# A state-space and attention kernel: another order of PSUM banks, copies and softplus steps in its projection stage

## The chip, the cores and the metric

The kernel runs on one core of one Trainium2 chip. The metric is the device time of one execution in microseconds (us), as the median of several. An execution handles a batch of four images.

## What is computed

Every image has 128 channels of 64 x 64 pixels, so 4096 tokens of 128 values. Layer 0 scores and sorts patches, then runs a selective state-space model over the sorted tokens; layer 1 is attention and a mixture of eight experts. The change lies in the first part of the state-space model:

```python
xz = x1n @ in_proj_w.T
xm, z = (xz[..., :D_INNER], xz[..., D_INNER:])            # D_INNER = 256
xp = jnp.pad(xm.transpose(0, 2, 1), ((0, 0), (0, 0), (D_CONV - 1, 0)))
xc = jax.lax.conv_general_dilated(xp, conv1d_w[:, None, :], (1,), 'VALID', ...)   # 4 taps per channel
xc = jax.nn.silu(xc + conv1d_b[None, :, None]).transpose(0, 2, 1)
dbc = xc @ x_proj_w.T
dt = jax.nn.softplus(dt_low @ dt_proj_w.T + dt_proj_b)
dBx = dt[..., None] * Bc[:, :, None, :] * xc[..., None]   # the kernel's u is dt * xc
```

`silu(z)` is wanted later and made here too. Softplus is made as relu(v) + log(1 + exp(-|v|)), with a correction for what is rounded away when 1 is added.

## The kernel before

The program is a loop over the four images. For each it runs stages that end in a barrier of all engines: `score_and_sort`, `project`, `scan`, `unsort`, `qkv`, `attention`, `ffn`. A stage gives each engine its own list of instructions, executed in order; semaphores tie the lists together, and nothing reorders them. The change is in `project` (L631) and in one new helper.

`project` cuts the 4096 tokens into eight chunks of 512 columns. The 256 inner channels are two halves of 128 partitions, so most steps occur twice per chunk (`h` = 0, 1):

- TensorE: `inproj(c)` (L654) makes two matmuls for x into PSUM banks 0 and 1 and two for z into banks 2 and 3. `xproj(c)` (L647) makes two accumulating matmuls into bank 4. The trace lists an f32 matmul of this size as two passes, so a pair as four.
- ScalarE: `keep_xi(c)` (L677) copies the x banks into `xi` in SBUF, `silu_z(c)` (L688) makes Silu out of the z banks, `silu_x(c)` (L682) makes Silu of the convolved chunk, and `keep_dbc(c)` (L693) copies bank 4 into `dbc`. Before, the order is `keep_xi(c)`, `silu_x(c-1)`, `silu_z(c)`, `keep_dbc(c-1)`.
- VectorE: `convolve(c)` (L729) makes the four taps of each half, two multiplies (L735) and six multiply-adds (L738).

Each bank is reused for each chunk, so `inproj(c)` waits for the copies of chunk c-1 out of the same banks, and VectorE waits for the copies of its chunk.

For the first chunk only, the stage also makes what the scan needs at once. These steps are the methods of `Steps` (L535). ScalarE rounds a part of `dbc` ("high", L592, and "middle", L596), between which GpSimd makes the remainder (L611) and "low" (L615). TensorE makes the dt matmuls of both halves (`tensor_dt`, L568) into banks 5 and 6; ScalarE makes absolute value and Relu of each (L575, L576), the exponential (L580), adds one (L585), and, behind VectorE's `vector_rounding` (L601), the logarithm (L589). GpSimd then makes three sums and products of 1024 columns (`pool_softplus`, L621, L625, L628). Exp, Ln and Silu need different function tables of ScalarE; each switch is an `ACT_TABLE_LOAD`, some placed by `ready_table` (L103). Before, "high" stands behind chunk 1, "middle" behind chunk 2, the block from the table load to adding one behind chunk 3, and the logarithm behind chunk 5. The later chunks' softplus is made within the scan, with the same helpers, and is not changed.

```python
def body(c):
    keep_xi(c)
    silu_x(c - 1)
    silu_z(c)
    keep_dbc(c - 1)
```

Of the kernel before, what the change touches and what calls it, by code (L numbers as in the profile page):

```python
# [15 lines left out]
DI, DS, DR, DC = 2 * C, 16, C // 16, 4  # L16
HD = DI // 128
# [610 lines left out]
            pool.tensor_tensor(halves(self.u[q]), halves(self.dt[q]), self.xc[:, :, cols_of(c)], ALU.mult).then_inc(self.dt_s, 1)  # L628


def project(k):  # L631


    steps = Steps(k, (5, 6))
    nc = k.nc
    x1 = k.at(X1_AT, L)
    xc = k.at(XC_AT, HD * L).rearrange("p (h n) -> p h n", h=HD)
# [6 lines left out]
    with nc.Block() as block:  # L644
        @block.tensor
        def _(pe):
            def xproj(c):  # L647
                pe.wait_ge(xc_s, c * HD + HD)
                pe.wait_ge(xp_ev, c + 1)
                for h in range(HD):  # L650
                    last = pe.matmul(k.bank(4), k.xpw[:, h, :], xc[:, h, cols_of(c)], start=h == 0, stop=h == HD - 1)
                last.then_inc(xp_mm, 1)

            def inproj(c):  # L654
                for h in range(HD):
                    pe.wait_ge(xi_ev, c * HD + (h + 1))
                    pe.matmul(k.bank(h), k.wx[:, h * 128:(h + 1) * 128], x1[:, cols_of(c)], start=True, stop=True).then_inc(xi_mm, 1)
                for h in range(HD):
                    pe.wait_ge(z_ev, c * HD + (h + 1))
                    pe.matmul(k.bank(2 + h), k.wz[:, h * 128:(h + 1) * 128], x1[:, cols_of(c)], start=True, stop=True).then_inc(z_mm, 1)  # L660
# [12 lines left out]
            xproj(NCH - 1)  # L673

        @block.scalar
        def _(act):
            def keep_xi(c):  # L677
                for h in range(HD):
                    act.wait_ge(xi_mm, c * HD + (h + 1))
                    act.activation(xi[:, h, cols_of(c, CH, DC - 1)], k.bank(h), ACT.Copy).then_inc(xi_ev, 1)  # L680

            def silu_x(c):  # L682
                for h in range(HD):
                    act.wait_ge(tap_s, c * (HD * DC) + (HD * (DC - 1) + h + 1))
                    act.activation(xc[:, h, cols_of(c)], xc[:, h, cols_of(c)], ACT.Silu,
                                   bias=k.cols[:, C_CB + h:C_CB + h + 1]).then_inc(xc_s, 1)

            def silu_z(c):  # L688
                for h in range(HD):
                    act.wait_ge(z_mm, c * HD + (h + 1))  # L690
                    act.activation(sz[:, h, cols_of(c)], k.bank(2 + h), ACT.Silu).then_inc(z_ev, 1)

            def keep_dbc(c):  # L693
                act.wait_ge(xp_mm, c + 1)
                act.activation(dbc[:, cols_of(c)], k.bank(4), ACT.Copy).then_inc(xp_ev, 1)

            for s, n in ((xi_ev, HD), (z_ev, HD), (xp_ev, 1)):
                act.sem_inc(s, n)
            def body(c):
                keep_xi(c)  # L700
                silu_x(c - 1)
                silu_z(c)
                keep_dbc(c - 1)
# [15 lines left out]
            with act.Fori(4, NCH - 2) as c:  # L719
                body(c)  # L720
            steps.scalar_log(act, 0)
            body(NCH - 2)
            body(NCH - 1)
            silu_x(NCH - 1)
            keep_dbc(NCH - 1)

        @block.vector
        def _(dve):
            def convolve(c):  # L729
                dve.wait_ge(xi_ev, c * HD + (2 * HD))  # L730
# [971 lines left out]
```

## Time and profile before

| | us |
|---|---|
| median of 3 executions | 5907.59 (5905.54 to 5909.15) |
| the profiled execution, its own time | 5915.02 |
| its span in the profile | 5913.3 |
| VectorE busy in the span | 5095.8 (86%) |
| TensorE busy | 4687.3 (79%) |
| ScalarE busy | 3659.2 (62%) |
| GpSimd busy | 1753.6 (30%) |

Engines are PE (TensorE), PEld (its weight loads), DVE (VectorE), ACT (ScalarE), POOL (GpSimd) and SP (the DMA queue's engine). A line number such as L738 is that of the kernel before. In a timeline, consecutive like instructions are merged into one row: its start, the time from the first start to the last end, and in brackets the idle time of the engine before it with what ended it. Instructions of one engine may overlap by their latency, so the distance between two starts can be shorter than a duration.

### The profile page before, as it was taken

The page shows a single profiled execution, that of the slowest core. Times are in us where ns is not written, and L with a number is a line of the kernel's source. Part 1 is how long each engine was busy: PE and PEld are TensorE (multiplying, and loading weights), DVE is VectorE, ACT ScalarE, POOL GpSimd, SP SyncE. Part 2 cuts the span into 40 slices and gives each one's busy share as a digit, 9 for nine tenths or more (in the row PEclk, how much of TensorE's full clock was granted, in tenths as well). Part 3 has the DMA queues.
Part 4 walks back from the last instruction along what each step waited for, and adds up shares of the span by engine and source line. Part 5 has one row for each costly group of instructions (what it writes and reads, how often), then busy time and mean ns, then how long its engine had stood idle before and what let it go on. Part 6 is the DMA issues. An engine that isn't in the chain of part 4 may idle for free. (4 is left out here: it accounts for less than half of the span.)

```text
span 5913.3 us, 100635 instructions
## 1 busy us (share of the span) xinstructions
PE 4687.3 (79%) x33816; PEld 1950.2 (33%) x33880; DVE 5095.8 (86%) x6562; ACT 3659.2 (62%) x4769; POOL 1753.6 (30%) x1306
## 2 busy tenths in 40 slices
PE   5776779998667777999866677799986667779997
PEld 2222433333322243333432224333343222433334
DVE  6799769998779977999877997799986899679998
ACT  1666458883266646888326663688922666368892
POOL 3388600000148860000014885000001488500000
PEclk9899989999889998999888999899988899989998
DMA  1000020000000002000000000200000000020000
GB/s 38 0 1 0 15 62 9 9 5 22 22 0 1 0 15 62 9 9 5 22 22 0 1 0 15 62 9 9 5 22 22 0 1 0 15 62 9 9 5 15
DMA packets 41626, 87.14 MB, mean 15 GB/s; under 512 B 11672, under 2 KB 27872, under 8 KB 38112
## 3 DMA queue, kind: packets, MB, share of 16 engines
q1 hardware_dynamic: 41184, 81.11, 5.1%
q8 instruction: 294, 4.82, 0.3%
q14 instruction: 148, 1.21, 0.1%
HBM read 26.55 MB, written 8.39 MB: 6 GB/s over the span
## 5 line engine op out<-in xcount | busy, mean ns | idle before, releaser
L1271 ACT ACTIVATE arena<-ps 128x1024 f32<-128x1024 f32 x2048 | 1913.2, 1027 | 266.8 <-PE ps L1236 246.4
L1286 DVE TENSOR_TENSOR arena<-arena 128x1024 f32<-128x1024 f32 x1664 | 1904.7, 1216 | 42.7 <-ACT arena L1271 40.6
L916 DVE TENSOR_TENSOR_SCAN arena<-ps,hlast,arena 128x512 f32<-128x512 f32 x1024 | 1258.4, 1264 | 5.2 <-DVE arena L898 3.2
L876 POOL TENSOR_TENSOR arena<-arena 128x1024 f32<-128x1024 f32 x512 | 1206.3, 2356 | 22.6
L1236 PE MATMUL ps<-arena 128*32 128x512 f16 x16384 | 1096.7, 384 | 118.1 <-issue 92.9
L1219 PE MATMUL ps<-arena 128*32 128x512 f32 x8192 | 1079.6, 605 | 45.9 <-DVE arena L1291 38.1
L845 ACT ACTIVATE ps<-arena,amat 128x512 f32<-128x512 f32 x1024 | 691.9, 688 | 506.9 <-DVE arena L916 506.1
L813 PE MATMUL ps<-arena,ident 128*128 128x512 f32 x2048 | 973.1, 598 | 7.7 <-POOL arena L876 7.7
L1594 POOL MEMSET arena<- 128x1024 f32 x4 | 3.8, 956 | 2688.1 <-POOLq L101 2688.1
L1236 PEld LDWEIGHTS ps<-arena 128*32 128x32 f16 x16384 | 471.4, 98 | 974.3 <-issue 696.7
L898 DVE TENSOR_TENSOR arena<-arena,ps 128x1024 f32<-128x1024 f32 x512 | 609.9, 1191 | 50.3 <-remote 32.3
L813 PEld LDWEIGHTS ps<-arena,ident 128*128 128x128 f32 x2048 | 392.3, 193 | 344.9 <-issue 270.7
L821 PE MATMUL ps<-arena,sel 128*128 128x512 bf16 x448 | 178.7, 399 | 410.8 <-DVE arena L898 410.8
L1219 PEld LDWEIGHTS ps<-arena 128*32 128x32 f32 x8192 | 212.3, 109 | 467.5 <-ACT arena L1271 239.1
L821 PEld LDWEIGHTS ps<-arena,sel 128*128 128x128 bf16 x512 | 49.8, 97 | 802.8 <-DVE arena L898 747.1
L848 ACT ACTIVATE arena<-ps 128x512 f32<-128x512 f32 x512 | 297.6, 581 | 21.2 <-PE ps L825 20.4
L825 PE MATMUL ps<-arena,sel 128*128 128x512 bf16 x512 | 200.7, 392 | 101.5 <-ACT arena L576 41.5
L1640 DVE SCALAR_TENSOR_TENSOR arena<-ps,arena 128x128 f32<-128x128 f32 x1024 | 274.3, 342 | 1.6 <-PE ps L1545 0.3
L1545 PE MATMUL ps<-expw,arena 128*128 128x512 f32 x512 | 250.6, 615 | 11.1 <-DVE arena L1609 8.3
L462 PE MATMUL ps<-arena 128*128 128x512 f32 x512 | 233.7, 616 | 18.3 <-DVE arena L349 18.3
L873 POOL COPY hlast<-arena 128x2 f32<-128x2 f32 x512 | 117.1, 229 | 317.0 <-DVE arena L916 317.0
L1208 PE MATMUL ps<-arena,ones 128*32 128x512 f32 x1536 | 204.3, 604 | 3.1 <-DVE arena L1286 2.0
(242 smaller groups left out, 4409.5 us busy)
## 6 DMA issues: line engine op xcount, KB each, us to landing
arena<-x SPq DMA_DIRECT2D x32, 512.0 KB, 5.5
arena<-arena SPq DMA_DIRECT2D x64, 256.0 KB, 6.0
arena<-arena SPq DMA_DIRECT2D x64, 224.0 KB, 5.8
arena<-arena SPq DMA_DIRECT2D x28, 512.0 KB, 3.4
arena<-pe SPq DMA_DIRECT2D x256, 32.0 KB, 1.8
out<-arena SPq DMA_DIRECT2D x8, 1024.0 KB, 3.9
expw<-L_ffn_expert_w SPq DMA_DIRECT2D x1, 512.0 KB
wqkv<-L_attn_W_qkv SPq DMA_DIRECT2D x1, 192.0 KB
```

What stands on the lines that cost most here:

```text
L813: last = pe.matmul(k.bank(Y_BANK + h), k.ident[:, :], halves(g[s % 4])[:, h, :], start=False, stop=s == DS - 1)
L845: act.activation(da(s, h), halves(dt[q])[:, h, :], ACT.Exp, scale=k.amat[:, h, s:s + 1]).then_inc(da_s, 1)
L848: act.activation(cs[s % 4], k.bank(C_BANK), ACT.Copy).then_inc(cs_s, 1)
L876: pool.tensor_tensor(halves(g[s % 4]), halves(hb[s % 4]), cs[s % 4].unsqueeze(1).broadcast_to([128, HD, CH]), ALU.mult).then_inc(hc_s, 1)
L898: dve.tensor_tensor(halves(dbx[s % 2]), halves(u[q]), k.bank(B_BANK).unsqueeze(1).broadcast_to([128, HD, CH]), ALU.mult).then_inc(dbx_s, 1)
L916: dve.tensor_tensor_scan(halves(hb[s % 4])[:, h, :], da(s, h), halves(dbx[s % 2])[:, h, :], k.hlast[:, s, h, :], ALU.mult, ALU.add).then_i ...
L1219: last = pe.matmul(k.ps[32 * h:32 * h + 32, O * CH:(O + 1) * CH], v[:, j * 128 + 32 * h:j * 128 + 32 * h + 32], probs[(2 * j + h // 2) % 8 ...
L1236: last = pe.matmul(k.ps[32 * t:32 * t + 32, (2 * group[p] + e) * CH:(2 * group[p] + e + 1) * CH], ks[:, h, j * 128 + 32 * t:j * 128 + 32 * ...
L1271: act.activation(probs[p % 8], k.bank(2 * group[p], 2 * CH), ACT.Exp, scale=SCALE / SPLIT ** 2).then_inc(exp_s, 1)
L1286: dve.tensor_tensor(acc[p % 2], acc[p % 2], probs[p % 8], ALU.add).then_inc(acc_s, 1)
L1545: pe.matmul(k.bank(expert_bank(i, hb)), tnt[:, i * 128:(i + 1) * 128], k.expw[:, hb * HE:hb * HE + HE, :].rearrange("p e c -> p (e c)"), s ...
L1640: dve.scalar_tensor_tensor(tile, k.bank(expert_bank(i, hb), C, e * C), gate[:, i, hb * HE + e:hb * HE + e + 1], tile, ALU.mult, ALU.add).t ...
```

## The change

In `project`, TensorE's banks are given anew: the x matmuls alternate between two pairs of banks (0, 1 and 2, 3), z has 4 and 5, the x-projection 6, and both dt matmuls 7, the second behind the Relu of the first. ScalarE copies the x banks of chunk c+3 where it copied those of chunk c+1; all of the first chunk's softplus steps on ScalarE stand together behind the copy of chunk 5. The three last softplus steps go from GpSimd to VectorE, behind its eighth chunk; the rounding step stands behind chunk 5 where it stood behind chunk 4. The credits that ScalarE gave at the start go, and all loops over chunks are written out.

```diff
+    def vector_softplus(self, dve, c, q):
+        dve.wait_ge(self.ln_s, c + 1)
+        dve.tensor_tensor(self.onep, self.onep, self.ab, ALU.subtract).then_inc(self.l1_s, 1)
+        dve.wait_ge(self.l1_s, c + 1)
+        dve.wait_ge(self.rx_s, c * 2 + 2)
+        dve.tensor_tensor(self.dt[q], self.onep, self.rx, ALU.add).then_inc(self.dt_s, 1)
+        dve.wait_ge(self.dt_s, c * 2 + 1)
+        dve.tensor_tensor(halves(self.u[q]), halves(self.dt[q]), self.xc[:, :, cols_of(c)], ALU.mult).then_inc(self.dt_s, 1)
...
-    steps = Steps(k, (5, 6))
+    XI_BANK, Z_BANK, XP_BANK, DT_BANK = 0, 4, 6, 7
+    steps = Steps(k, (DT_BANK, DT_BANK))
...
-            inproj(0)
-            for c in range(1, 4):
-                inproj(c)
-                xproj(c - 1)
-                if c == 2:
-                    pe.wait_ge(xp_ev, 2)
+            inproj_x(0)
+            inproj_x(1)
+            inproj_z(0)
+            for c in range(2, NCH):
+                inproj_x(c)
+                if c == 5:
+                    pe.wait_ge(xp_ev, 1)
                     for h in range(HD):
+                        if h:
+                            pe.wait_ge(steps.rx_s, h)
                         steps.tensor_dt(pe, 0, h)
-            with pe.Fori(4, NCH) as c:
-                inproj(c)
-                xproj(c - 1)
+                inproj_z(c - 1)
+                xproj(c - 2)
+            inproj_z(NCH - 1)
+            xproj(NCH - 2)
             xproj(NCH - 1)
...
             keep_xi(0)
+            keep_xi(1)
             silu_z(0)
-            body(1)
-            act.wait_ge(xp_ev, 2)
+            keep_xi(2)
+            silu_x(0)
+            silu_z(1)
+            keep_xi(3)
+            keep_dbc(0)
+            silu_x(1)
+            silu_z(2)
+            keep_xi(4)
+            keep_dbc(1)
+            silu_x(2)
+            silu_z(3)
+            keep_xi(5)
+            act.wait_ge(xp_ev, 1)
             steps.scalar_high(act, 0, 0)
-            body(2)
-            steps.scalar_middle(act, 0, 0)
-            body(3)
             k.ready_table(act, ACT.Exp, 1)
             for h in range(HD):
                 steps.scalar_abs(act, 0, h)
+            steps.scalar_middle(act, 0, 0)
             steps.scalar_exp(act, 0)
             steps.scalar_one_plus(act, 0)
+            steps.scalar_log(act, 0)
             k.ready_table(act, ACT.Silu, 2)
...
+            for c in range(3, NCH):
+                keep_dbc(c - 1)
+                silu_x(c)
+                if c < NCH - 1:
+                    silu_z(c + 1)
+                if c + 3 < NCH:
+                    keep_xi(c + 3)
             keep_dbc(NCH - 1)
...
-            with dve.Fori(0, 5) as c:
+            for c in range(NCH):
                 convolve(c)
-            steps.vector_rounding(dve, 0)
-            with dve.Fori(5, NCH) as c:
-                convolve(c)
+                if c == 5:
+                    steps.vector_rounding(dve, 0)
+            steps.vector_softplus(dve, 0, 0)
...
-            for part in range(3):
-                if part == 2:
-                    steps.pool_wait(pool, xc_s, HD)
-                steps.pool_softplus(pool, 0, 0, part)
```

In the changed kernel the copies are L703, Silu of x L708, Silu of z L714, the keep of `dbc` L718; the x matmuls L672, those of z L679, the x-projection L665; the taps L762 and L765.

ScalarE before, from the keep of `dbc` of chunk 2 to the end of the block:

```order
L695 ACTIVATE arena<-ps 128x512
L107 ACT_TABLE_LOAD
L107 ACTIVATE small<-ones 128x1
L575 ACTIVATE arena<-ps,cols 128x512
L576 ACTIVATE arena<-ps,cols 128x512
L575 ACTIVATE arena<-ps,cols 128x512
L576 ACTIVATE arena<-ps,cols 128x512
L580 ACTIVATE arena<-arena 128x1024
L585 ACTIVATE arena<-arena,cols 128x1024
L107 ACT_TABLE_LOAD
L107 ACTIVATE small<-ones 128x1
```

and the logarithm before, between the keep of chunk 4 and the Silu of chunk 5:

```order
L589 ACT_TABLE_LOAD
L589 ACTIVATE arena<-arena 128x1024
L680 ACTIVATE arena<-ps 128x512 x2
L685 ACT_TABLE_LOAD
L685 ACTIVATE arena<-arena,cols 128x512 x2
```

ScalarE in the changed kernel, from "middle" to the copies of chunk 6:

```order
L596 ACTIVATE arena<-arena 64x512
L580 ACTIVATE arena<-arena 128x1024
L585 ACTIVATE arena<-arena,cols 128x1024
L589 ACT_TABLE_LOAD
L589 ACTIVATE arena<-arena 128x1024
L107 ACT_TABLE_LOAD
L107 ACTIVATE small<-ones 128x1
L718 ACTIVATE arena<-ps 128x512
L708 ACTIVATE arena<-arena,cols 128x512 x2
L714 ACTIVATE arena<-ps 128x512 x2
L703 ACTIVATE arena<-ps 128x512 x2
```

"Middle" and the logarithm have moved into the block, one table load has gone, and the copies of chunk 6 stand behind the block and the Silu of chunk 3.

TensorE in the changed kernel, from the x matmuls of chunk 5 to the z matmuls of chunk 5 (wx: x, wz: z, xpw: x-projection, dtw: dt):

```order
L672 MATMUL ps<-arena,wx 128x512 x2
L568 MATMUL ps<-arena,dtw 128x512 x2
L679 MATMUL ps<-arena,wz 128x512 x2
L665 MATMUL ps<-arena,xpw 128x512 x2
L672 MATMUL ps<-arena,wx 128x512 x2
L679 MATMUL ps<-arena,wz 128x512 x2
```

The dt matmuls have moved from behind the x-projection of chunk 1 to the place behind the x matmuls of chunk 5, and the x-projection here is that of chunk 3, ahead of the x matmuls of chunk 6.

VectorE in the changed kernel, from the rounding step to the end of the stage:

```order
L601 SCALAR_TENSOR_TENSOR arena<-arena 128x1024
L762 TENSOR_SCALAR arena<-arena,taps 128x512 x2
L765 SCALAR_TENSOR_TENSOR arena<-arena,taps 128x512 x6
L762 TENSOR_SCALAR arena<-arena,taps 128x512 x2
L765 SCALAR_TENSOR_TENSOR arena<-arena,taps 128x512 x6
L635 TENSOR_TENSOR arena<-arena 128x1024
L638 TENSOR_TENSOR arena<-arena 128x1024
L640 TENSOR_TENSOR arena<-arena 128x1024
```

Two chunks stand behind the rounding instead of three, and the three steps that were GpSimd's come last.

## Rows read from the trace of the kernel before

**Rows 1.** The page's costliest groups: busy us, mean ns, idle before and releaser
```profile
L1286 DVE TENSOR_TENSOR arena<-arena 128x1024 f32<-128x1024 f32 x1664 | 1904.7, 1216 | 42.7 <-ACT arena L1271 40.6
```

**Rows 2.** The stage in each image: busy PE, PEld, DVE, ACT, POOL; clock
```profile
158.90:229.90 71.00, 51.79 (x100) 20.34 (x100) 45.48 (x66) 45.08 (x72) 11.75 (x7) 0.86 0.00 0
1629.50:1700.20 70.70, 51.41 (x100) 20.22 (x100) 45.47 (x66) 45.13 (x72) 11.75 (x7) 0.88 0.00 0
3104.60:3175.50 70.90, 51.75 (x100) 20.33 (x100) 45.47 (x66) 45.09 (x72) 11.74 (x7) 0.86 0.00 0
4575.60:4646.60 71.00, 51.85 (x100) 20.34 (x100) 45.45 (x66) 45.08 (x72) 11.74 (x7) 0.86 0.00 0
```

**Rows 3.** Timeline of VectorE, image 1: start us, us, what, count, idle before
```profile
163.36 0.88 DVE L735 TENSOR_SCALAR arena<-arena,taps  x2 [4.36 <-ACT arena L680]
...
168.13 0.87 DVE L735 TENSOR_SCALAR arena<-arena,taps  x2
...
193.19 0.88 DVE L735 TENSOR_SCALAR arena<-arena,taps  x2 [7.47 <-ACT arena L680]
...
209.03 2.04 DVE L735 TENSOR_SCALAR arena<-arena,taps  x2 [2.55 <-ACT arena L680]
211.00 8.26 DVE L738 SCALAR_TENSOR_TENSOR arena<-arena,taps  x6
```

**Rows 4.** Timeline of ScalarE, image 1
```profile
163.17 1.28 ACT L691 ACT_TABLE_LOAD   x1
164.47 1.08 ACT L691 ACTIVATE arena<-ps 128x512 f32<-128x512 f32 x2
...
177.14 0.62 ACT L596 ACTIVATE arena<-arena 64x512 bf16<-64x512 f32 x1
...
186.56 0.68 ACT L576 ACTIVATE arena<-ps,cols 128x512 f32<-128x512 f32 x1
...
188.27 1.07 ACT L580 ACTIVATE arena<-arena 128x1024 f32<-128x1024 f32 x1
189.37 1.15 ACT L585 ACTIVATE arena<-arena,cols 128x1024 f32<-128x1024 f32 x1
...
199.99 0.60 ACT L680 ACTIVATE arena<-ps 128x512 f32 x1 [1.12 <-PE ps L657]
...
206.82 1.06 ACT L589 ACTIVATE arena<-arena 128x1024 f32<-128x1024 f32 x1
...
210.16 1.33 ACT L685 ACTIVATE arena<-arena,cols 128x512 f32<-128x512 f32 x2
...
213.65 0.60 ACT L695 ACTIVATE arena<-ps 128x512 f32<-128x512 f32 x1 [1.19 <-PE ps L651]
...
215.37 0.60 ACT L680 ACTIVATE arena<-ps 128x512 f32<-128x512 f32 x1 [0.26 <-PE ps L657]
...
228.27 0.60 ACT L695 ACTIVATE arena<-ps 128x512 f32<-128x512 f32 x1 [2.60 <-PE ps L651]
```

**Rows 5.** Timeline of TensorE, image 1
```profile
194.36 3.77 PE L651 MATMUL ps<-arena,xpw 128*128 x4 [7.00 <-ACT arena L685]
197.93 2.78 PE L657 MATMUL ps<-arena,wx 128*128 x4
...
211.63 1.98 PE L651 MATMUL ps<-arena,xpw 128*128 x4 [3.42 <-ACT arena L685]
213.45 1.88 PE L657 MATMUL ps<-arena,wx 128*128 x4
...
220.15 3.67 PE L651 MATMUL ps<-arena,xpw 128*128 x4 [3.10 <-ACT arena L685]
```

**Rows 6.** Busy time as in rows 2, granted clock 0.69, a stretch of image 1
```profile
188.00:192.00 4.00, 0.00 (x0) 0.00 (x0) 0.00 (x0) 3.94 (x6) 0.00 (x0) 0.69 0.00 0
```

**Rows 7.** Timeline of GpSimd, image 1
```profile
177.94 1.72 POOL L615 TENSOR_TENSOR arena<-arena 32x512 bf16<-32x512 f32 x1 [3.94 <-ACT arena L596]
...
208.05 2.35 POOL L621 TENSOR_TENSOR arena<-arena 128x1024 f32<-128x1024 f32 x1 [28.40 <-ACT arena L589]
```

More of the change, by code:

```diff
@@ L648, in xproj, with inproj_x @@
                 pe.wait_ge(xc_s, c * HD + HD)
-                pe.wait_ge(xp_ev, c + 1)
+                if c >= 1:
+                    pe.wait_ge(xp_ev, c)
                 for h in range(HD):
-                    last = pe.matmul(k.bank(4), k.xpw[:, h, :], xc[:, h, cols_of(c)], start=h == 0, stop=h == HD - 1)
+                    last = pe.matmul(k.bank(XP_BANK), k.xpw[:, h, :], xc[:, h, cols_of(c)], start=h == 0, stop=h == HD - 1)
                 last.then_inc(xp_mm, 1)
-            def inproj(c):
+            def inproj_x(c):
@@ L655, in inproj @@
                 for h in range(HD):
-                    pe.wait_ge(xi_ev, c * HD + (h + 1))
-                    pe.matmul(k.bank(h), k.wx[:, h * 128:(h + 1) * 128], x1[:, cols_of(c)], start=True, stop=True).then_inc(xi_mm, 1)
-                for h in range(HD):
-                    pe.wait_ge(z_ev, c * HD + (h + 1))
-                    pe.matmul(k.bank(2 + h), k.wz[:, h * 128:(h + 1) * 128], x1[:, cols_of(c)], start=True, stop=True).then_inc(z_mm, 1)
-            inproj(0)
-            for c in range(1, 4):
-                inproj(c)
-                xproj(c - 1)
-                if c == 2:
-                    pe.wait_ge(xp_ev, 2)
+                    if c >= 2:
+                        pe.wait_ge(xi_ev, (c - 2) * HD + h + 1)
@@ new lines, in inproj_x, with inproj_z @@
+                    pe.matmul(k.bank(XI_BANK + HD * (c % 2) + h), k.wx[:, h * 128:(h + 1) * 128], x1[:, cols_of(c)],
+                              start=True, stop=True).then_inc(xi_mm, 1)
+            def inproj_z(c):
+                for h in range(HD):
+                    if c >= 1:
+                        pe.wait_ge(z_ev, (c - 1) * HD + h + 1)
+                    pe.matmul(k.bank(Z_BANK + h), k.wz[:, h * 128:(h + 1) * 128], x1[:, cols_of(c)], start=True, stop=True).then_inc(z_mm, 1)
+            inproj_x(0)
@@ L679, in keep_xi @@
                     act.wait_ge(xi_mm, c * HD + (h + 1))
-                    act.activation(xi[:, h, cols_of(c, CH, DC - 1)], k.bank(h), ACT.Copy).then_inc(xi_ev, 1)
+                    act.activation(xi[:, h, cols_of(c, CH, DC - 1)], k.bank(XI_BANK + HD * (c % 2) + h), ACT.Copy).then_inc(xi_ev, 1)
             def silu_x(c):
@@ L690, in silu_z @@
                     act.wait_ge(z_mm, c * HD + (h + 1))
-                    act.activation(sz[:, h, cols_of(c)], k.bank(2 + h), ACT.Silu).then_inc(z_ev, 1)
+                    act.activation(sz[:, h, cols_of(c)], k.bank(Z_BANK + h), ACT.Silu).then_inc(z_ev, 1)
             def keep_dbc(c):
                 act.wait_ge(xp_mm, c + 1)
[L695 to L703, printed above, removed]
+                act.activation(dbc[:, cols_of(c)], k.bank(XP_BANK), ACT.Copy).then_inc(xp_ev, 1)
             keep_xi(0)
+            keep_xi(1)
             silu_z(0)
-            body(1)
-            act.wait_ge(xp_ev, 2)
+            keep_xi(2)
[11 more added lines that the diff above has]
+            act.wait_ge(xp_ev, 1)
             steps.scalar_high(act, 0, 0)
-            body(2)
-            steps.scalar_middle(act, 0, 0)
-            body(3)
             k.ready_table(act, ACT.Exp, 1)
@@ L715, in _ @@
                 steps.scalar_abs(act, 0, h)
+            steps.scalar_middle(act, 0, 0)
             steps.scalar_exp(act, 0)
             steps.scalar_one_plus(act, 0)
+            steps.scalar_log(act, 0)
             k.ready_table(act, ACT.Silu, 2)
[L719 to L724, printed above, removed]
+            for c in range(3, NCH):
[5 more added lines that the diff above has]
+                    keep_xi(c + 3)
             keep_dbc(NCH - 1)
@@ L729, in convolve @@
             def convolve(c):
-                dve.wait_ge(xi_ev, c * HD + (2 * HD))
+                dve.wait_ge(xi_ev, c * HD + HD)
                 for t in range(DC):
```

## The prediction

> **What bounds the kernel now.** I read the page's costliest groups first. Attention leads: its additions alone hold VectorE for 1904.7 us [rows 1], and the change does not touch them. It rewrites one stage, projection, that runs once per image. The busy time of each engine by stage gives that stage's length in the four images: 71.0, 70.7, 70.9 and 71.0 us, together 283.6 us of the 5913.3 us span [rows 2]. No engine works there for more than 51.9 us (TensorE), VectorE and ScalarE for 45 us each. So the stage is bound by a chain that passes between engines, and the change can move tens of us at most.
>
> The timeline of image 1 shows that chain. One chunk (512 tokens) costs VectorE 4.77 us, from 163.36 to 168.13 [rows 3], so eight need 38 us; but VectorE waits for its copies, longest 7.47 us before chunk 4 [rows 3]. ScalarE does the softplus preparation in that gap, the exponential from 188.27 for instance [rows 4], and TensorE stands still for 7.00 us [rows 5]. Its granted clock falls to a mean of 0.69 between 188 and 192 us [rows 6], on the way from the upper of its two levels (2.4 GHz) to the lower (1.2 GHz). The next pair (a projection of one chunk, listed as four passes) takes 3.77 us where it takes 1.98 at full clock, and the pair behind it 2.78 [rows 5]. A second loss is at chunk 6. GpSimd's three softplus sums, the first of 2.35 us, begin at 208.05 [rows 7], and beside them VectorE's two multiplies take 2.04 and its six multiply-adds 8.26 us: 10.2 us for a chunk of 4.77 [rows 3].
>
> **The change, part by part.** Times are on image 1's clock; the stage begins at 158.9 as before.
>
> 1. *Credits and loops.* ScalarE's opening credits go, and all loops are written out. I take nothing for both; the bound is one hand-off between engines, 0.26 us [rows 4], either way, about 1 us in four images. Longer straight code could cost fetches; no row shows one, and what would cover it is VectorE's slack, on ScalarE nothing.
>
> 2. *First half, copies three chunks ahead.* The table load behind chunk 0's copies, 1.28 us at 163.17, moves behind chunk 1's two copies and ends near 166.0, with two Silus of z (1.08) behind it [rows 4]. TensorE's x-pair of chunk 2 is its third from 162.4, and pairs follow each other in 1.82 (211.63 to 213.45) [rows 5], so its copies are made near 168, when VectorE's taps of chunk 0 end too. Silu of chunk 0 starts at 168.2. From there a cycle repeats: Silu to its x-projection 1.47 (210.16 to 211.63), from there 3.74 to the second copy of the chunk three ahead (215.37), then the slot of that copy and of the keep of dbc, 0.49 each (a pair of 1.08 less one of 0.60) [rows 4, 5]: **6.19 us**. Silus of chunks 0, 1, 2 start at 168.2, 174.4 and 180.6; the copy of chunk 5 is done at 186.3. VectorE, with 4.77 per chunk, is never kept waiting and ends chunk 5 at 192.0. The four banks let the copies be early, but the cycle is longer than VectorE's chunk: ScalarE and TensorE in turn are what is late next.
>
> 3. *The softplus block, in one piece.* "High" (about 0.5), the Exp table load (1.28) and its warm-up (0.1) take ScalarE to 188.2. Both halves now share one bank. Abs and Relu take 0.57 each (186.56 to 188.27 is three of them) [rows 4], the second half's matmul waits for the first Relu (189.5), and ScalarE waits 1.2 us for it, until 190.6; before, it waited for nothing. Abs and Relu again, "middle" at 191.7, the exponential 192.2 to 193.3 (1.10). Adding one waits for GpSimd's "low", which starts 0.80 behind "middle" and takes 1.72 [rows 4, 7]: 194.3, a wait of 1.0 that was hidden before. Add one to 195.5 (1.15), VectorE's rounding 1.22 (as a 1024-column addition) [rows 1], the log 196.9 to 197.9, its table load hidden in that wait, the Silu table 1.4. ScalarE is free at **199.25**: 12.95 us. Before, the same work held ScalarE for 11.8 us in pieces: four table loads of 1.28, two warm-ups of 0.1, four times 0.57, then 1.10, 1.15, 0.96 for the log, and 1.0 for "high" and "middle". One of the four loads goes, and new waits take that back and 1.2 us more. The rows show a load as 1.28 us with the next activation 0.02 behind it [rows 4]. The Trainium skill ("ScalarE: Activation LUTs", What ACT_TABLE_LOAD costs) charges about 2.66 us per switch, a drain included. By that price the load that goes would be worth 1.38 us more per image, and the forecast would be 5.5 us lower; the rows show no such drain.
>
> 4. *Behind the block.* VectorE has no copy of chunk 6 and waits from 196.7. ScalarE's Silu of chunk 3 starts at 199.75, the x-projection at 201.2. TensorE will have been idle for some 9 us, more than the 7.00 that cost it the clock, so I take the rows at the low clock: 3.57 (194.36 to 197.93), then 2.06 to the first copy (199.99) [rows 4, 5] and 0.86 to the second, at 207.7. Silu of chunk 4 starts at 208.7, of chunk 5 at 214.9 (6.19 on). There are no copies left behind chunk 7's, so the last steps are Silu to keep, 1.47 + 2.02 (211.63 to 213.65), and the slot, 0.49: 3.98 each [rows 4, 5]. Silu of chunk 6 starts at 218.9, of chunk 7 at 222.8, and the last keep ends at **226.9**. Before it ended at 228.27 + 0.60 = 228.87 [rows 4]. Gain: **1.94 us**.
>
> 5. *Softplus sums on VectorE.* Three additions or products of 1.22 us [rows 1], 0.2 for the wait between them, stand behind chunk 7 (done near 218.9) and end by 223.1, hidden by ScalarE with almost 4 us to spare. Without that cover they cost 4.2. That GpSimd leaves chunk 6 alone gives VectorE 5.4 us back, but VectorE waits longer than that for the copy: worth nothing by itself.
>
> Sum: image 1's stage takes 71.0 - 1.94 = 69.06 us, four of them 276.2 instead of 283.6: **7.4 us** less. The profiled execution's 5915.0 becomes 5907.6. The median of the runs shown, 5907.59, lies 7.4 below that execution, so the forecast for it is **5900.2 us**.
>
> **The rivals.** About 0.2%, 11.8 us, is what a measurement of this kernel can tell from no change.
>
> *Faster: the clock is kept, or returns at once.* Then the pair behind the block takes 1.82 and the copies come after 1.92, 2.75 us less per image than in point 4: 7.4 + 11.0 = 18.4 us, 5889.2. Half of that passes 11.8 us. For it: the clock outlasted 3.42 us of idleness before 211.63, whose pair took 1.98 [rows 5]. Against it: 7.00 us were too long.
>
> *Slower: the clock stays low through the second half.* TensorE now works in bursts with a short wait before each x-projection. At the low clock a pair costs 1.75 more. From copy 6 on the path holds 0.85 and five such pairs: 9.6 us per image, 7.7 net, 31 in all, 5938. It turns slower than 0.2% from the fourth slow pair on (11.8 us in four images, over the 1.94 gained, is 4.9). For it: behind 3.10 us of idleness at 220.15 a pair took 3.67 [rows 5]. Against it: a cycle holds some 5.4 us of matmul in 6.19, denser than the stretch around 211.63, which kept its clock. The Trainium skill ("TensorE: Matmul & The Clock Gate", A second HAM failure mode: psum-queue depth-cycling) says that cycling through PSUM banks leaves small idle times between groups of matmuls in which the clock oscillates. By that rule it would be 5938; the row at 211.63 speaks against it.
>
> *No gain: single losses of the clock.* The matmul at 189.5 comes behind 3.0 us of idleness (x-projection 182.1, x-pair 183.9, first dt matmul 185.7 to 186.5); at the low clock it adds 0.85. The last x-projection, behind 2.1, adds up to 1.75, copy 6 another 0.85. All of them in every image: 3.45 - 1.94 = 1.5 us each, 5913.6.
>
> *The change does less than it says.* Copies three ahead are had for chunks up to 5 only; 6 and 7 wait for the softplus block. That follows from the order alone and is in the sum.
>
> **How the numbers follow.** A gain of 2 to 11.8 us: 0.53. No gain or a small loss: 0.14. The faster rival, whole or half: 0.27. The slower one: 0.06. The range reaches from the whole faster rival to most of the third one's: 5889 to 5912. So faster by over 0.2% gets 0.27, within it 0.67, slower 0.06.
>
> **What would show it.** In the changed trace the Silus of chunks 0, 1, 2 start 6.2 us apart; ScalarE waits 1.2 us before the second Abs and 1.0 before adding one; the block lasts 13 us; VectorE waits some 11 us before chunk 6, and no chunk takes it over 4.8; the pair behind the block takes about 3.8; the last keep ends 68 us behind the stage's start, with the sums wholly before it. The forecast is wrong if something other than the last keep holds the barrier, if the pair behind the block takes 1.98, or if pairs behind copy 6 take over 3.

## The result, and the profile after

The changed kernel takes 5917.97 us (median of 20 executions), the kernel before 5908.52 us beside it. Their ratio is 1.0017, with a 95% interval of 1.0011 to 1.0023: **slower by 10 us**, where 7.4 us less was forecast, and outside the range of 5889 to 5912. (One of the twenty executions, of 6621 us, fell into a slower state of the chip and is left out of the ratio.) The profiled execution took 5921.40 us, its span is 5919.7 us.

The busy time of each engine in the projection stage of each image, to set against [rows 2], gives what the stage now takes:

```profile
158.80:228.40 69.60, 49.88 (x100) 19.28 (x98) 43.21 (x68) 43.58 (x72) 8.41 (x5) 0.88 0.00 0
1632.90:1701.90 69.00, 51.05 (x100) 19.90 (x99) 43.21 (x68) 43.53 (x72) 8.31 (x5) 0.88 0.00 0
3104.30:3173.20 68.90, 50.89 (x100) 19.97 (x99) 43.22 (x68) 43.58 (x72) 8.36 (x5) 0.88 0.00 0
4578.60:4647.60 69.00, 51.05 (x100) 19.90 (x98) 43.22 (x68) 43.52 (x72) 8.29 (x5) 0.88 0.00 0
```

From each start to the last keep of `dbc` and the barrier behind it the stage now takes 69.6, 69.0, 68.9 and 69.0 us, 276.5 in all; 276.2 was forecast, and it was 283.6. Against this one profile the gain of 7 us is there.

**The gain is smaller than that.** In four of the experiments below, TensorE, ScalarE and GpSimd have the stage's old code. From the first x matmul to GpSimd's first instruction of the scan, the four images sum there to 272.8, 276.6, 279.6 and 281.8 us, and to 283.4 in the profile of before: 278.8 on average. The six profiles with the changed kernel's order, that one's included, have 276.0 to 276.6. So what the change gains in this stage is some 2.4 us on average. An image of the old order takes either 67.4 to 67.6 us (6 of 20) or 69.7 to 71.0. The first image of the kernel before with only VectorE's loops written out:

```profile
158.00:225.50 67.50, 49.27 (x100) 19.47 (x100) 45.77 (x66) 45.28 (x72) 11.78 (x8) 0.90 0.00 0
```

and its TensorE:

```profile
158.01 1.98 PE L657 MATMUL ps<-arena,wx 128*128 128x512 f32 x4 [2.20 <-ACTq L698]
...
207.98 3.12 PE L651 MATMUL ps<-arena,xpw 128*128 x4 [3.42 <-ACT arena L685]
...
216.47 1.98 PE L651 MATMUL ps<-arena,xpw 128*128 x4 [1.38 <-ACT arena L685]
```

where the profile of before has, for the first pair,

```profile
158.93 3.59 PE L657 MATMUL ps<-arena,wx 128*128 128x512 f32 x4 [2.20 <-ACTq L698]
```

and 1.98 and 3.67 for the other two [rows 5]. TensorE's code is the same, and so is the 3.42 us of idleness before the second of them; the low stretches of its clock fall elsewhere.

The whole became 10 us slower, so there must be a loss in another stage. The same view over the attention stage, whose code the change does not touch, first of the kernel before:

```profile
823.80:1383.70 559.90, 527.72 (x6553) 183.60 (x6554) 517.98 (x449) 483.73 (x520) 0.00 (x0) 0.98 0.05 13
2297.10:2860.20 563.10, 531.71 (x6550) 184.74 (x6543) 519.70 (x449) 483.65 (x520) 0.00 (x0) 0.97 0.05 13
3767.90:4328.30 560.40, 528.04 (x6553) 183.89 (x6554) 517.39 (x449) 483.91 (x520) 0.00 (x0) 0.98 0.05 13
5239.20:5799.50 560.30, 527.96 (x6553) 183.93 (x6554) 517.37 (x449) 483.87 (x520) 0.00 (x0) 0.98 0.05 13
```

and of the changed kernel:

```profile
823.00:1385.30 562.30, 531.38 (x6554) 183.52 (x6555) 519.45 (x449) 484.12 (x520) 0.00 (x0) 0.98 0.05 13
2295.70:2859.70 564.00, 534.11 (x6554) 185.07 (x6555) 519.87 (x449) 484.16 (x520) 0.00 (x0) 0.97 0.05 13
3767.00:4331.00 564.00, 533.57 (x6554) 183.71 (x6555) 519.88 (x449) 484.10 (x520) 0.00 (x0) 0.97 0.05 13
5242.00:5805.50 563.50, 532.29 (x6550) 183.78 (x6543) 519.48 (x449) 484.23 (x520) 0.00 (x0) 0.98 0.05 13
```

Attention grew from 2243.7 to 2253.8 us, the scan from 2040.6 to 2043.3; the feed-forward stage adds 1.9. So the two profiled executions differ by -7.1 + 10.1 + 2.7 + 1.9, and -1.2 in the other stages: +6.4 us of span.

**Where attention lost it.** At the end of each of its 32 chunks (8 per image) VectorE takes the reciprocal of the sums and then multiplies by it; TensorE waits for the product. One such place in VectorE's timeline before (start, us, what, idle before):

```profile
3906.43 3.36 DVE L1288 RECIPROCAL arena<-ps 128x512 f32<-128x512 f32 x1 [1.33 <-PE ps L1208]
3910.05 0.69 DVE L1291 TENSOR_TENSOR arena<-ps,arena 128x512 f32 x1 [0.26 <-DVE arena L1288]
```

and after:

```profile
3904.77 3.36 DVE L1311 RECIPROCAL arena<-ps 128x512 f32<-128x512 f32 x1 [1.32 <-PE ps L1231]
3908.50 0.69 DVE L1314 TENSOR_TENSOR arena<-ps,arena 128x512 f32 x1 [0.38 <-DVE arena L1311]
```

The two instructions take as long as before, but 0.38 us lie between them where 0.26 did. It is 0.35 to 0.38 in 28 of the 32 places; in the first chunk of each image it is 0.61, where it was 0.26 as well:

```profile
895.70 0.69 DVE L1314 TENSOR_TENSOR arena<-ps,arena 128x512 f32 x1 [0.61 <-DVE arena L1311]
```

The profile's view of the product's line in the kernel before sums this over all chunks: who kept it waiting, and who waited for it (us, times):

```profile
  DVE arena L1288: 8.2, 32
...
  PE ps L1219: 38.1, 28
```

and in the changed kernel:

```profile
  DVE arena L1311: 12.6, 32
...
  PE ps L1242: 42.1, 28
```

12.6 - 8.2 = 4.4 us of VectorE, and TensorE waits 42.1 - 38.1 = 4.0 us longer. TensorE's matmuls also took longer: in the four windows it was busy for 2115.4 us before and for 2131.3 after, for the same matmuls. Its timeline behind this product before:

```profile
3910.79 1.92 PE L1219 MATMUL ps<-arena 128*32 128x512 f32 x16 [1.34 <-DVE arena L1291]
```

and after:

```profile
3909.24 2.72 PE L1242 MATMUL ps<-arena 128*32 128x512 f32 x12 [1.47 <-DVE arena L1314]
```

Sixteen passes took 1.92 us at the upper level (2.4 GHz); here twelve take 2.72, at 1.2 GHz. The granted clock of the windows is lower in image 3 (0.97 for 0.98), but one execution of each is too little to size that.

### The profile page after: what moved, and what is told of

It is laid out like the page before. It is cut to its first block and busy times, and to the rows that moved or that the text cites. A ratio compares the mean times of both kernels' runs of the same rounds, so it can differ in the third digit from the quotient of the medians.

```text
span 5919.7 us, 99875 instructions
## 1 busy us (share of the span) xinstructions
PE 4728.7 (80%) x33880; PEld 1954.5 (33%) x33880; DVE 5095.4 (86%) x6574; ACT 3654.3 (62%) x4765; POOL 1742.2 (29%) x1294
## 5 line engine op out<-in xcount | busy, mean ns | idle before, releaser
L1242 PE MATMUL ps<-arena 128*32 128x512 f32 x8192 | 1094.5, 613 | 50.6 <-DVE arena L1314 42.1
L844 PE MATMUL ps<-arena,sel 128*128 128x512 bf16 x512 | 204.5, 399 | 430.5 <-DVE arena L921 417.1
L1568 PE MATMUL ps<-expw,arena 128*128 128x512 f32 x512 | 251.8, 618 | 10.1 <-DVE arena L1632 8.3
L848 PE MATMUL ps<-arena,sel 128*128 128x512 bf16 x512 | 201.1, 393 | 58.1 <-ACT arena L576 36.3
```

The costliest lines, as they stand in the source:

```text
L844: pe.matmul(k.bank(B_BANK), k.sel[:, s, :], pieces[q], start=True, stop=True).then_inc(b_mm, 1)
L1242: last = pe.matmul(k.ps[32 * h:32 * h + 32, O * CH:(O + 1) * CH], v[:, j * 128 + 32 * h:j * 128 + 32 * h + 32], probs[(2 * j + h // 2) % 8 ...
```

## The experiments

**Theory A**: the written-out loops and the three softplus steps made VectorE's list longer, and some place in that list at a fixed distance from its start costs about 0.1 us (a pause) whenever it is passed. The new length puts it between attention's reciprocal and product, on the path. **Rivals**: the loss comes from what the stage does (its steps or its end) and would stay with another length; or it is chance between executions. Ratios are to the kernel before on the same chip, five rounds each.

### VectorE's taps in loops again

```diff
-            for c in range(NCH):
+            with dve.Fori(0, 6) as c:
+                convolve(c)
+            steps.vector_rounding(dve, 0)
+            with dve.Fori(6, NCH) as c:
                 convolve(c)
-                if c == 5:
-                    steps.vector_rounding(dve, 0)
```

> The changed kernel, with VectorE's eight tap chunks as two hardware loops again (0 to 5, 6 and 7); nothing else differs. Theory A (length of VectorE's program): the projection stage stays at 69 us an image, VectorE's idle time between reciprocal and product in attention falls from 0.38 back to 0.26 us, attention falls from 562 to 564 us to about 560, and the whole to 5900 to 5908. Theory B (chance position of the clock's low stretches only): 0.38 and 5912 to 5924 stay. Theory C (the new order of banks and copies costs something behind the stage): the same numbers as B.

Measured: 5899.05 against 5903.36 us, ratio 0.9998 (0.9989 to 1.0007). The sums at the product are back at 8.2 and 38.1 us. The projection stage stays at 276.2 us. Attention took 2219.7 us; its first window, shorter than the 560 expected:

```profile
825.50:1378.30 552.80, 523.29 (x6553) 182.29 (x6546) 517.77 (x449) 484.12 (x520) 0.00 (x0) 0.99 0.05 13
```

Theory A held. The data instructions are the same; only the form of the list differs, with the register operations that a loop needs. But the kernel is now only as fast as the one before, not the forecast 7 us faster.

### The kernel before with its tap loops written out

```diff
-            with dve.Fori(0, 5) as c:
-                convolve(c)
-            steps.vector_rounding(dve, 0)
-            with dve.Fori(5, NCH) as c:
+            for c in range(NCH):
                 convolve(c)
+                if c == 4:
+                    steps.vector_rounding(dve, 0)
```

> The kernel before, with only VectorE's tap loops written out; bank, copy order and softplus as before. Theory A: the idle time between reciprocal and product becomes 0.38 us, 32 times 0.12 to 0.14 us, so 4 us at least, and with more low-clock stretches in attention up to 16: 5912 to 5925. Theories B and C: 0.26 and 5903 to 5912, as before.

Measured: 5904.34, ratio 1.0004 (0.9995 to 1.0014), and the place stayed at 0.26 us. A miss: writing the loops out is not enough by itself. It has to be the right number of instructions.

### One instruction more in the changed kernel, fifteen more in the one before

An instruction that does nothing of use, in VectorE's setup ahead of all stages; here one of them, in the other kernel 15:

```diff
+            for i in range(1):
+                dve.memset(k.at(i, 1), 0.0)
```

> The changed kernel, with one memset of one column more on VectorE in the setup, under 0.1 us once, so that everything behind it on VectorE stands one instruction later. By my count of the programs the product stands 15 instructions later in the changed kernel than before; with this one 16. Theory A in the form 'position within a block of instructions': 0.26 us again, 5900 to 5908. Theory A in the form 'sheer length', B and C: 0.38, 5912 to 5924.

> The kernel before, with fifteen such memsets in the setup, about 1 us once. Theory A, position: 0.38 us between reciprocal and product, attention 2 to 4 us longer an image, 5913 to 5925. B and C: 0.26 and 5904 to 5913.

Measured: 5915.61, ratio 1.0023 (1.0013 to 1.0032), with one; 5905.01, ratio 1.0001 (0.9992 to 1.0010), with fifteen. Both expectations missed, because I had the distance wrong, and both taught it. In the first the pause stayed (12.8 us over 32 chunks) but moved: it lies ahead of the small register operation that precedes the product (which starts 3.60 us behind the reciprocal's start, 3.49 in the changed kernel), where in the changed kernel it lies behind it. In the second the product is undisturbed, and the pause stands two instructions behind it, at the branch of the loop (3.82 us behind the reciprocal's start, 3.71 in the kernel before). There it takes the same 4.4 us of VectorE in 32 passes, and the kernel is no slower for it. Counted in the lists, the changed kernel lies 17 places further than the one before, so 17 should hit and 8 more than the changed one should be clear.

### Eight more in the changed kernel, seventeen in the one before

The same edit with `range(8)` in the changed kernel, `range(17)` in the one before.

> The changed kernel with eight one-column memsets in VectorE's setup. In the runs so far a delay of 0.1 us sits at one place of VectorE's list and moves one instruction ahead for each that is added: before the product in the changed kernel, one instruction ahead of it with one pad, two behind it in the kernel before with fifteen pads. Eight pads put it ahead of the reciprocal, where VectorE waits for TensorE anyway. Theory A (position): idle time between reciprocal and product 0.26 us, attention 8 to 15 us shorter in four images than in the changed kernel, 5893 to 5904 in all, which is the projection stage's own 7 us under the kernel before. Theory B/C (the order of banks and copies has the price): 0.26 perhaps, but 5912 to 5920.

> The kernel before with seventeen such memsets, which puts the delay at the place that it has in the changed kernel. Theory A: idle time 0.37, four-image attention 4.4 us longer at the least, and with the clock's share 12: 5908 to 5918. Theories B and C: like the kernel before, 5900 to 5906.

Measured: the changed kernel with eight takes 5901.13, ratio 0.9996 (0.9987 to 1.0005). The kernel before with seventeen takes 5917.08, ratio **1.0021** (1.0010 to 1.0031), as slow as the change, without any of its steps. The product's line in the kernel before with seventeen:

```profile
  DVE arena L1290: 12.6, 32
...
  PE ps L1221: 42.1, 28
```

and in the changed kernel with eight:

```profile
  DVE arena L1313: 8.2, 32
...
  PE ps L1244: 38.1, 28
```

With eight more, the pause is still in the loop. It stands ahead of the last addition before the reciprocal, and there too it takes 4.4 us in 32 passes, but VectorE then waits for TensorE anyway. This settles the main cause: adding instructions turned the loss on in a kernel that has nothing of the change, and off in the one that has all of it. Without the loss the changed kernel's gain can't be told from nothing: ratio 0.9996 here and 0.9998 with the loops. The forecast 7.4 us would be 0.9987, at the lower end of one interval and just below the other.

### A control: eight more in the kernel before

> Control: the kernel before with eight one-column memsets on VectorE in the setup, 0.5 us once. The delay is then nine instructions behind where seventeen pads put it, outside the stretch from reciprocal to product: idle time 0.26 and no change against the kernel before, 5899 to 5906. If pads have a price of their own, 5908 or more.

Measured: 5906.30, ratio 1.0005 (0.9996 to 1.0014); the place at 8.2 and 38.1 us. Such instructions cost nothing that can be measured, unless they move the pause to where it counts. Against this control, the seventeen cost 0.0021 - 0.0005 = 0.16%, some 9 us; against the changed kernel with eight, the change's own list costs 0.17 + 0.04 = 0.21%, 12 us. From the intervals of the ratios, each is uncertain by 0.11 to 0.14%.

Of these 9 to 12 us, 4.4 are the pause. The other thing seen to differ is TensorE's clock, and its share is not shown. From attention's first matmul to VectorE's first instruction behind it, the four images sum to:

| | with the pause at the product | without |
|---|---|---|
| old order of the projection stage | 2249.8 us | 2237.5 to 2247.3, mean 2242.9 (4 profiles) |
| new order | 2247.0 and 2252.5 | 2219.8 to 2236.3, mean 2229.1 (7 profiles) |

The clock stood at its lower level there for 98 to 114 us with the pause, without it for 95 to 119 us in the old order and 61 to 87 us in the new one. So in the old order the profiles show no more low clock with the pause than without, and in the new order they do. They also show attention some 14 us shorter behind the new order than behind the old, both without the pause, though its code is the same. No experiment says why.

### The sums on GpSimd again

```diff
                     steps.vector_rounding(dve, 0)
-            steps.vector_softplus(dve, 0, 0)
...
             steps.pool_low(pool, 0, 0)
+            for part in range(3):
+                if part == 2:
+                    steps.pool_wait(pool, xc_s, HD)
+                steps.pool_softplus(pool, 0, 0, part)
```

> The changed kernel with the three softplus sums on GpSimd again. By my steps the sums would run in VectorE's wait for the copy of chunk 6 (from 197 to 205 us, chunk 6 starts at 207) and collide with nothing: the projection stage stays at 69.1 us an image. A rival (the collision with chunk 6 stays, as before) gives VectorE a chunk of 8 to 10 us and a stage of 71 to 73. VectorE's list is three instructions shorter, so the delay should fall two or three behind the product; idle time 0.26, whole 5893 to 5906.

Measured: 5897.44, ratio 0.9989 (0.9981 to 0.9998), the place at 0.257 us, the projection stages 276.4 us. GpSimd's timeline, image 1:

```profile
199.39 2.34 POOL L621 TENSOR_TENSOR arena<-arena 128x1024 f32<-128x1024 f32 x1 [3.79 <-ACT arena L589]
...
204.53 2.34 POOL L628 TENSOR_TENSOR arena<-arena 128x1024 f32<-128x1024 f32 x1 [0.18 <-POOL arena L625]
```

and VectorE's:

```profile
210.02 4.06 DVE L765 SCALAR_TENSOR_TENSOR arena<-arena,taps 128x512 f32<-128x512 f32 x6
```

The sums end at 206.87, before VectorE has chunk 6 to work on, so the collision of before (8.26 us for the multiply-adds, [rows 3]) is gone without VectorE taking them. That part of the change is worth nothing that can be measured (0.9989 here, 0.9996 with the sums on VectorE, and the intervals overlap), and the shorter list of VectorE has no pause on the path.

### What holds the softplus block

In the changed kernel GpSimd's subtraction took 6.17 us beside VectorE's taps (below). Two kernels: one with only the PSUM banks for dt changed, back to two of them (the second is one of the x banks, so TensorE waits for both Relus before chunk 6's x matmuls); and one with that together with remainder and "low" on VectorE, between the taps, the rounding ahead of chunk 5, and ScalarE's "high" and "middle" ahead of the block.

```diff
-    steps = Steps(k, (DT_BANK, DT_BANK))
+    steps = Steps(k, (DT_BANK, XI_BANK))
...
                         if h:
-                            pe.wait_ge(steps.rx_s, h)
+                            pe.wait_ge(xi_ev, 4 * HD + 1)
```

and for the second kernel also, with "high" behind the Silu of z of chunk 2 and "middle" behind that of chunk 3 (not shown),

```diff
                 convolve(c)
-                if c == 5:
+                if c == 2:
+                    steps.vector_remainder(dve, 0, 0)
+                if c == 4:
+                    steps.vector_low(dve, 0, 0)
                     steps.vector_rounding(dve, 0)
```

> The changed kernel with eight pads and only the second dt matmul in bank 0, so that it follows the first at once. ScalarE's wait of 1.2 us before the second Abs goes. But 'middle' waits for GpSimd's remainder, which ends when VectorE has ended chunk 5 (190.9 us in the changed kernel), so if that wait is what ends last, nothing is gained: stage 69.0. If the Abs wait is on the path: 67.8 and 5896 in all. I expect 69.0 and 5898 to 5904.

> The changed kernel with 'high' and 'middle' in ScalarE's waits for the copies of chunks 4 and 5, remainder and 'low' on VectorE behind chunks 2 and 4, the rounding ahead of chunk 5, and the second dt matmul in bank 0, so that it waits for no Relu. Worked out from the changed kernel's rows: 1.2 us of wait for the second Abs, 1.25 and 0.5 for GpSimd, and 1.0 for the two roundings leave the softplus block, so the stage is 3.9 to 4.4 us shorter an image, 65 us. With the delay of VectorE's list out of the way (its place is only known once it runs): 5880 to 5892. If the block is not on the path: 5896 to 5906.

Measured with the bank alone (and eight instructions more, to keep the pause away): 5900.49, ratio 0.9993 (0.9984 to 1.0002), stages of 69.0 us, as without it. ScalarE's timeline says why:

```profile
193.86 0.63 ACT L598 ACTIVATE arena<-arena 64x512 bf16<-64x512 f32 x1 [2.56 <-POOL arena L613]
```

The 1.22 us that it no longer waits before the second Abs it waits longer for GpSimd: 2.56 where it was 1.25. With the GpSimd steps on VectorE and "high" and "middle" moved as well: **5885.10, ratio 0.9968 (0.9955 to 0.9981)**, stages of 65.1, 62.5, 65.3 and 65.2 us. Its ScalarE runs through the block without a wait:

```profile
189.74 0.69 ACT L576 ACTIVATE arena<-ps,cols 128x512 f32<-128x512 f32 x1
190.31 1.07 ACT L580 ACTIVATE arena<-arena 128x1024 f32<-128x1024 f32 x1
```

and VectorE pays little for it:

```profile
178.08 0.68 DVE L634 TENSOR_TENSOR arena<-arena 64x512 f32<-64x512 f32 x1
...
188.22 0.67 DVE L639 TENSOR_TENSOR arena<-arena 32x512 bf16<-32x512 f32 x1
```

A subtraction that took GpSimd 6.17 us takes VectorE 0.68. The stage is 3.7 to 3.9 us shorter than with the bank alone in three images, near the 3.9 to 4.4 expected, and 6.5 in the second; which of the moved steps brings how much was not measured apart.

### The same with the sums on GpSimd

> The eighth kernel with the three softplus sums on GpSimd again, three instructions fewer on VectorE. The sums fit into VectorE's wait before chunk 6 (198 to 205 us), so the stage stays at 65.2 us: 5881 to 5890, if the delay in VectorE's list does not fall between reciprocal and product; 5893 to 5905 if it does (0.37 us there).

Measured: 5883.48, ratio 0.9969 (0.9957 to 0.9981), stages 65.2, 62.5, 65.1 and 62.5 us. (Its pause is at the branch of attention's loop, where it costs nothing.) No difference from the one above that can be told; both beat the kernel before by 18 us.

### Why the scan gives something back

From GpSimd's first instruction of a scan to the end of VectorE's last `TENSOR_TENSOR_SCAN`, the four images sum to 1879.6 to 1883.4 us in the five kernels whose stage ends as before (the one before, and it with its loops written out or with 8, 15 or 17 instructions more), and to 1886.8 to 1890.2 us in all eight with the new order. That is some 6 us more, over twice the 2.4 that the stage gains. Nothing in the scan's code differs. Theory D: it is the moment at which the scan starts, not the steps, that matters. Two ScalarE copies that nothing needs, behind the last keep of the changed kernel with eight:

```diff
             keep_dbc(NCH - 1)
+            act.activation(k.at(42496, 1024), k.at(41472, 1024), ACT.Copy)
+            act.activation(k.at(43520, 512), k.at(41472, 512), ACT.Copy)
```

> The changed kernel with eight pads (5901.1 us) and two more copies on ScalarE behind its last keep of dbc, 1024 and 512 columns into columns that nothing uses, 1.5 us; the projection stage ends 1.5 us later, near 70.5 us. In all kernels with the new copy order the scan behind the stage takes 510.9 to 511.4 us an image instead of 509.1, and so returns most of what the stage gained. Theory D (the scan's 2 us hang on when it starts): it falls to 509 to 510 and the whole stays at 5901. Theory E (they hang on the shorter stage in no such way): the scan stays at 511 and the whole is 5905 to 5909.

Measured: 5895.69, ratio 0.9989 (0.9980 to 0.9998): the whole was expected at 5901 and came out lower, faster than its twin (ratio 0.9996) by work that is of no use, though their intervals overlap. The scan of image 2 in the twin:

```profile
1697.80:2208.70 510.90, 368.50 (x970) 157.44 (x971) 464.32 (x400) 302.29 (x470) 397.49 (x299) 0.97 0.01 5
```

and here:

```profile
1697.30:2206.80 509.50, 365.13 (x970) 156.14 (x971) 464.17 (x400) 302.49 (x470) 397.80 (x299) 0.97 0.01 5
```

The scan stages take 2037.0 us for 2046.4, with PE busy for 365 to 366 us where it was 368 to 373 for the same count of matmuls: TensorE loses less of its clock. By the measure above they take 1880.9, as in the kernels of the old order, and 6 to 9 us less than in the eight others of the new one. So the scan fell as Theory D said, in this one kernel; other starts were not tried.

## Why the prediction was wrong

**Step 1 failed: "Longer straight code could cost fetches; no row shows one, and what would cover it is VectorE's slack."** I looked for the cost in the stage that the change touches, where VectorE has slack. The cost of a longer list fell behind that stage, in attention, where VectorE and TensorE wait for each other at each chunk's end. I took nothing for it, 1 us at most; it cost 9 to 12 us, of which 4.4 are the pause itself. The rows of before could not show where the pause would fall, and bad luck had a part: with a list eight instructions longer, or without the three sums, it costs nothing. That lists grow ahead of a place with no slack could be seen, and should have been a rival. That the pause is a fetch is not shown: the rows show an idle 0.11 us (0.36 at the loop's first pass in each image) at a place that moves with the number of instructions ahead of it. The Trainium skill ("Advanced Engine Details and Errata", ISA Cache) says that an engine's instruction cache has two lines of 256 instructions each. That could fit a pause at a fixed distance; no run here measured the distance between two of them, so the trace neither bears it out nor speaks against it.

**The sum was too large: "four of them 276.2 instead of 283.6: 7.4 us less".** The 276.2 came out (276.5), the 283.6 was one profile. Its 3.67 us for the pair of chunk 6 [rows 5], and the slow first pair, were carried as fixed, and neither is there in every execution: five profiles of the old order average 278.8, so 2.4 us are gained. I also put nothing for the stages behind, and the scan takes some 6 us more behind the new order. Without the pause, 5901.13 lies near the forecast 5900.2 for the kernel before at 5907.6, but the kernel before took 5902.41 beside it: that nearness is luck.

**Step 2 held.** The Silus of chunks 0, 1 and 2, forecast 6.19 us apart, are 6.08 and 6.09 apart. ScalarE, image 1:

```profile
159.59 0.60 ACT L703 ACTIVATE arena<-ps 128x512 f32<-128x512 f32 x1 [2.07 <-PE ps L672]
...
166.09 1.32 ACT L708 ACTIVATE arena<-arena,cols 128x512 f32<-128x512 f32 x2
...
172.17 1.33 ACT L708 ACTIVATE arena<-arena,cols 128x512 f32<-128x512 f32 x2
...
178.26 1.33 ACT L708 ACTIVATE arena<-arena,cols 128x512 f32<-128x512 f32 x2
...
188.38 0.69 ACT L575 ACTIVATE arena<-ps,cols 128x512 f32<-128x512 f32 x1 [1.22 <-PE ps L568]
...
190.89 0.63 ACT L596 ACTIVATE arena<-arena 64x512 bf16<-64x512 f32 x1 [1.25 <-POOL arena L611]
...
192.94 1.15 ACT L585 ACTIVATE arena<-arena,cols 128x1024 f32<-128x1024 f32 x1 [0.47 <-POOL arena L615]
...
197.88 0.58 ACT L718 ACTIVATE arena<-ps 128x512 f32<-128x512 f32 x1
...
221.38 1.32 ACT L708 ACTIVATE arena<-arena,cols 128x512 f32<-128x512 f32 x2
226.38 0.60 ACT L718 ACTIVATE arena<-ps 128x512 f32<-128x512 f32 x1 [3.69 <-PE ps L665]
```

They start 2.1 us early, at 166.09 instead of 168.2, since the first copies came faster (159.59, before 161.04): in this image the first pairs ran at the full clock. In images 2 to 4 they did not, and the first Silu starts 9.3 us behind the first matmul, as forecast (168.2 - 158.9). VectorE was not kept waiting up to chunk 5.

**Step 3: the block was 1 us longer, and one cause was another.** The wait of 1.22 us before the second Abs (188.38) is the 1.2 forecast. I had put 1.0 before adding one and nothing before "middle"; it is 1.25 before "middle" (190.89) and 0.47 before adding one (192.94). The block, from 183.88 to 197.88, lasted 14.0 us instead of 12.95. The term that I had at nothing is the wait for GpSimd's subtraction:

```profile
184.69 6.17 POOL L611 TENSOR_TENSOR arena<-arena 64x512 f32<-64x512 f32 x1 [24.92 <-ACT arena L592]
```

6.17 us, until 190.86; before, around a gap between two of VectorE's chunks (its multiply-adds ended at 172.97, the next began at 173.54), it took 1.50, from 172.49. VectorE was in its taps (chunk 5, to 189.85), and they took no longer:

```profile
185.79 4.06 DVE L765 SCALAR_TENSOR_TENSOR arena<-arena,taps 128x512 f32<-128x512 f32 x6
...
207.15 0.88 DVE L762 TENSOR_SCALAR arena<-arena,taps 128x512 f32<-128x512 f32 x2 [11.81 <-ACT arena L703]
```

So the same two engines that lost on VectorE's side in chunk 6 before ([rows 3]) lose on GpSimd's side here. The Trainium skill ("Advanced Engine Details and Errata", GPSIMD Details) says that the two share an interface to SBUF and conflict when VectorE reads two inputs there; the rows agree that they conflict (6.17 us for 1.50). Which of the two loses, the runs show but do not explain.

**Step 4 held, in image 1 partly by luck.** TensorE, image 1:

```profile
199.73 3.78 PE L665 MATMUL ps<-arena,xpw 128*128 128x512 f32 x4 [9.67 <-ACT arena L708]
...
214.97 1.98 PE L665 MATMUL ps<-arena,xpw 128*128 128x512 f32 x4 [0.68 <-ACT arena L708]
...
222.75 3.60 PE L665 MATMUL ps<-arena,xpw 128*128 128x512 f32 x4 [1.90 <-ACT arena L708]
```

The pair behind the block took 3.78 us (forecast 3.8) behind 9.67 of idleness, VectorE had waited 11.81 us for chunk 6 (forecast some 11), and all ran 1.4 us ahead of the forecast times up to Silu of chunk 7 (221.38 instead of 222.8). Then the last x-projection took 3.60 us at the low clock, one of the "single losses"; in images 2 to 4 it took 1.98. The last keep ended at 226.98 (forecast 226.9): in image 1 the 1.4 us of lead and this loss of 1.6 all but cancel. In images 2 to 4 neither is there, and the last keep ends 67.9 to 68.0 us behind the first matmul, as forecast.

**Step 5 held:** the sums on VectorE are worth nothing by themselves, as the kernel with them on GpSimd again shows.

**The rivals.** The faster one did not come about (3.78, not 1.98). The slower one did not either: pairs behind chunk 6's copies took 1.98, not 3.67, and of the "single losses" only the last x-projection's came, in one image of four. Idleness alone does not foretell the clock here: behind the same 3.42 us a pair took 1.98 us in the profile of before and 3.12 in the one with the loops written out, and behind 1.9 us it took 3.60 in image 1 and 1.98 in images 2 to 4. A slower kernel came, but by a mechanism that I had not named; the 0.06 had nothing of it.

**What stays open:** what makes the pause; what the 5 to 8 of the 9 to 12 us are that are not the pause itself, the clock being argued and not shown; why attention is shorter behind the new order; and which start of the scan suits it, and why.

## What to carry to other kernels

When an edit makes an engine's list longer or shorter, compare the stages that it does not touch as well: sum the small idle times at their tightest hand-offs, and if they moved, add a few empty instructions and measure again before judging the edit. A change of 0.2% can be nothing but this, as large as the gain that one looks for. Take more than one profile of the kernel before, too: the old order of the projection stage took from 272.8 to 283.4 us in five profiles, and a forecast gain of 7.4 us was 2.4. Between two engines that slow each other, look on which side of the meeting the critical path lies, and put the small steps on the engine that has them done quickest.

## What the runs showed of the hardware that was not expected

- An idle 0.11 us at one place of VectorE's list at each pass of a loop, 0.36 at the first pass of each image, that moves one instruction when one is added ahead. Between reciprocal and product it makes 8.2 us into 12.6 over 32 chunks and costs 9 to 12 us of the whole time; the same 4.4 us at the loop's branch or ahead of the last addition cost nothing.
- TensorE's clock in an unchanged stage: behind the same 3.42 us of idleness a pair of matmuls took 1.98 us in one kernel and 3.12 in another, and an image's projection took 67.4 to 71.0 us with the same steps.
- GpSimd's subtraction of 64 x 512 took 6.17 us beside VectorE's multiply-adds and 1.50 without them, while VectorE's kept their 4.06.
- Copies of no use, 1.5 us of ScalarE per image, shortened the four scans behind them by 6 to 9 us in all.
